# One kernel of four layers: tokens chosen and experts run in one stage, the first layer's products in three float32r passes, the second layer's output products in halves

## The reference, cut to what matters

```
L0:  v = x @ values (16 heads x 64);  cumv = cumsum(v over tokens)
     att = exp((x@aw - max) * temperature);  attn = att * cumv / (att * count + 1e-30)
     op = attn.reshape(S, 1024) @ operator + cond
     res = relu(concat[x, op] @ ff1 + b1) @ ff2 + b2 + x;   x = layernorm(res)
L1:  one-head attention over the normed and FiLM-scaled x, then an MLP of width 1024
L2:  16 heads of 16 features:  out = softmax(q k^T) v, projected, added; then a normed sum
L3:  16 heads of 64 features: attention; then a mixture of 8 experts:
     gate = softmax(tok @ Wgate);  vals, idx = top_k(gate.T, 256)     # each expert picks 256 tokens
     g = layernorm(tok[idx]);  y = gelu(g @ fc1[e] + b1[e]) @ fc2[e] + b2[e]
     tok[idx] += y * vals
```

## Time and profile before

| | us |
|---|---|
| median of 3 runs | 2302.05 (2297.03 to 2305.03) |
| the profiled execution | 2303.45 |
| its span, first to last instruction | 2301.7 |
| mean granted clock of PE over it | 0.897 |
| L0's chunks, about | 36 to 239 |
| L2 heads, about | 698 to 1090 |
| choice, about | 2054 to 2146 |
| experts, about | 2146 to 2302 |

### The profile page before, as it was taken

The page is one execution under the profiler, slowest core; times in us unless marked ns, Lnnn a source line. Parts: engine busy times, 40 slices in busy tenths (PEclk is TensorE's granted clock), DMA queues, the critical chain, the costliest instruction groups (busy, mean ns, idle before and its releaser), DMA issues. The chain is left out here.

```text
span 2301.7 us, 35109 instructions
## 1 busy us (share of the span) xinstructions
PE 1931.4 (84%) x13374; PEld 1181.4 (51%) x13374; DVE 1435.9 (62%) x2490; ACT 1116.1 (48%) x1909; POOL 739.2 (32%) x683
## 2 busy tenths in 40 slices
PE   6998589769747999998389949999999999794776
PEld 3444357658423333332267735555555555483676
DVE  5433453363338989991678857777777777218655
ACT  1111232232211878886167647777777777203242
POOL 2122350074003030000425544444444444103466
PEclk8999799979875999997689979999999999895688
DMA  5000000000133311100238873444444444342153
GB/s 161 0 1 0 16 7 1 22 17 1 37 110 83 89 41 50 47 23 8 80 103 254 261 196 85 111 111 111 111 111 111 111 111 111 97 166 86 36 161 80
DMA packets 196231, 190.99 MB, mean 83 GB/s; under 512 B 64416, under 2 KB 154912, under 8 KB 195808
## 3 DMA queue, kind: packets, MB, share of 16 engines
q1 hardware_dynamic: 192992, 184.56, 30.1%
q0 software_dynamic: 3072, 4.20, 0.9%
HBM read 121.07 MB, written 67.37 MB: 82 GB/s over the span
## 5 line engine op out<-in xcount | busy, mean ns | idle before, releaser
L1302 DVE TENSOR_REDUCE l3h_nmax<-l3h_score 128x1 f32<-128x1024 f32 x256 | 313.5, 1225 | 150.7 <-PE l3h_score L1245 150.6
L1336 POOL TENSOR_SCALAR l3h_prob<-l3h_prob,l3h_inv 128x1024 f32<-128x1024 f32 x256 | 287.0, 1121 | 341.8 <-DVE l3h_inv L1308 341.8
L1528 ACT ACTIVATE l2h_pT<-l2h_score 128x512 f32<-128x512 f32 x512 | 266.1, 603 | 119.2 <-PE l2h_score L1453 117.6
L1495 DVE TENSOR_REDUCE l2h_nm<-l2h_rowb 128x1 f32<-128x1024 f32 x256 | 301.2, 1218 | 35.9 <-PE l2h_rowb L1442 35.9
L1326 ACT ACTIVATE l3h_prob<-l3h_score,l3h_nmax 128x1024 f32<-128x1024 f32 x256 | 285.9, 1117 | 48.7 <-DVE l3h_nmax L1302 13.7
L1268 PE MATMUL l3h_out<-l3h_pT,l3h_vs 128*64 128x512 f32 x1024 | 274.4, 617 | 0.0
L1245 PE MATMUL l3h_score<-l3h_K,l3h_Q 64*128 64x512 f32 x1536 | 249.6, 431 | 23.7 <-DMA l3h_K<-l_k 21.9
L1245 PEld LDWEIGHTS l3h_score<-l3h_K,l3h_Q 64*128 64x128 f32 x1536 | 125.9, 187 | 235.4 <-issue 197.4
L1442 PE MATMUL l2h_rowb<-l2h_K,l2h_Q 48*128 48x512 f32 x512 | 185.9, 477 | 44.2 <-DMA l2h_K<-l_k 29.9
L1453 PE MATMUL l2h_score<-l2h_Q,l2h_K 50*128 50x512 f32 x512 | 204.1, 485 | 4.7 <-ACT l2h_pT L1528 4.7
L1294 ACT ACTIVATE l3h_pT<-l3h_ring 128x512 f32<-128x512 f32 x256 | 152.8, 597 | 101.4 <-PE l3h_ring L1256 100.9
(11 more groups left out here) (377 smaller groups left out, 3583.9 us busy)
## 6 DMA issues: line engine op xcount, KB each, us to landing
l3h_Q<-l_q SPq DMA_DIRECT2D x128, 256.0 KB
l3h_K<-l_k SPq DMA_DIRECT2D x128, 128.0 KB
l_v<-l3qkv_v SPq DMA_DIRECT2D x16, 512.0 KB, 4.3
l_q<-l3qkv_hi SPq DMA_DIRECT2D x16, 512.0 KB, 5.1
l_q<-l3qkv_lo SPq DMA_DIRECT2D x16, 512.0 KB, 4.4
l_k<-l3qkv_hi SPq DMA_DIRECT2D x16, 512.0 KB, 3.5
l_k<-l3qkv_lo SPq DMA_DIRECT2D x16, 512.0 KB, 3.3
l3h_vs<-l_v SPq DMA_DIRECT2D x32, 256.0 KB, 3.2
```

The lines of the kernel that those rows point to most:

```text
L1302: dve.tensor_reduce(self.nmax[:, t % 4:t % 4 + 1], self.score[t % 2][:, :], AX.X, ALU.max, negate=True).then_inc(self.maxes, 1)
L1336: pool.tensor_scalar(self.prob[:, q, :], self.prob[:, q, :], self.inv[:, q:q + 1], self.vscale, ALU.mult, ALU.mult).then_inc(self.scaled, 1)
L1495: dve.tensor_reduce(self.nm[:, mr % 2, at:at + 1], self.rowb[h][:, :], AX.X, ALU.max, negate=True).then_inc(self.maxes, 1)
L1528: act.activation(self.pT[:, g % 4, h, c * C:(c + 1) * C], self.score[v % 3][:, :], ACT.Exp).then_inc(self.exps, 1)
```

## The change

**L0.** `values`, the operator and the half of `ff1` that meets `oT` are split once into high and low parts, `csum` and `oT` once for each chunk, `aT` for each `j` (high part on ACT, low part on POOL); their products run in three passes. PE's order in a chunk is values(j), spread(j), operate(j-2), so the operator product runs in pieces inside the loop over `j`. The small sums for later layers come at j = 3, the second half of the cumulative sums on DVE at n = 5 and 6. `gam` and `bet` are applied chunk by chunk. The loads of the L2 weights move from L0 to `layer1_qkv`. Buffers share storage (`zero`, `sel32`, the raw weights).

**L2 heads.** For tiles 1 to 6, `mix` is done in two halves of 256 columns, one after each phase. Where there are no rows left, PE repeats a row product of the last pair (`again`); nothing reads it.

**Choice and experts** become one stage. One-hots and picks are made for three experts first and the others three experts ahead, inside the loop. Tokens are turned after the second pair of `up`, their high part is written by ACT from PSUM. Weight loads, semaphores and splits are separate for the two matrices, and the splits stand between the gelus. All sixteen biases are loaded once.

```diff
 # layer0, PE
+            for c in range(NC):
+                pe.wait_ge(chi, (c + 1) * KF)
+                pe.wait_ge(clo, (c + 1) * KF)
+                values(c, 0)
+                spread(c, 0)
+                for j in range(1, FT):
+                    values(c, j)
+                    spread(c, j)
+                    if j >= 2:
+                        operate(c, j - 2)
+                    if j == 3:
...
+                for j in range(FT - 2, FT):
+                    operate(c, j)
...
+                for m in range(KF):
+                    for k in range(KF):
+                        pe.matmul(bank[6 + m][:, :], ff1[:, k, m * P:(m + 1) * P], xT[:, k, cc], start=k == 0, stop=False)
+                pe.wait_ge(opc, (c + 1) * 2 * KF)
+                pe.wait_ge(ohi, (c + 1) * KF)
+                for m in range(KF):
+                    for k in range(KF):
+                        for p_, (x, y) in enumerate(PASSES):
+                            mm = pe.matmul(bank[6 + m][:, :], ff1o[x][:, k, m * P:(m + 1) * P], oTp[y][:, k, :],
 # layer0, DVE, in the loop over j
-                    dve.tensor_tensor(aT[:, j, :], bank[2 + n % 2][:, :], rb[:, n % 2, :], ALU.mult).then_inc(ats, 1)
+                    if n >= 2:
+                        dve.wait_ge(alo, n - 1)
+                        dve.wait_ge(ahi, n - 1)
+                    dve.tensor_tensor(aT[:, n % 2, :], bank[2 + n % 2][:, :], rb[:, n % 2, :], ALU.mult).then_inc(ats, 1)
 # NarrowPairs, PE
+            at, w = (part * C // 2, C // 2) if 0 < k < TB - 1 else (0, C)
...
-                    if phase == 0:
-                        mine, kk = (m, k - self.LAG) if k >= self.LAG else (m - 1, k - self.LAG + TB)
-                        if self.there(mine):
-                            mix(mine, kk)
+                    mine, kk = (m, k - self.LAG) if k >= self.LAG else (m - 1, k - self.LAG + TB)
+                    if self.there(mine) and (phase == 0 or 0 < kk < TB - 1):
+                        mix(mine, kk, phase)
 # experts, SP
+            for m in range(2):
+                ew.load(sp, 1, m)
+            for e in range(E):
+                sp.dma_start(b1[:, e, :], columns(w["b1"][e, :]), allow_slow_non_contiguous=True).then_inc(bl, 16)
+            for m in range(2):
+                ew.load(sp, 2, m)
             sp.wait_ge(normed, T)
             sp.dma_start(g["tokn"].rearrange("(t p) d -> p t d", p=P), xn[:, :, :]).then_inc(stored, 16)
             sp.wait_ge(stored, 32)
+            for e in range(E):
+                sp.dma_start(b2[:, e, :], rows(w["b2"][e, :])).then_inc(bl, 16)
+            ew.load(sp, 3, 0)
+            for e in range(3, E):
+                if e + 1 < E:
+                    ew.load(sp, e + 1, 0)
+                ew.load(sp, e, 1)
 # experts, PE
+            tokens(0)
             for e in range(E):
+                up(e)
+                if e >= 1:
+                    down(e - 1)
+                if e + AHEAD < E:
+                    pick(e + AHEAD)
+            down(E - 1)
 # experts, DVE
+                for q in range(PAIRS):
+                    dve.wait_ge(gelus, e * F + 2 * q + 2)
+                    dve.tensor_copy(yp[0][:, e % 2, 2 * q:2 * q + 2, :], y[:, 2 * q:2 * q + 2, :]).then_inc(yhs, 1)
+                    if q == 0 and e >= 1 and e + AHEAD - 1 < E:
+                        indices(e + AHEAD - 1)
+                    if q == 2 and e + 1 < E:
+                        tokens(e + 1)
+                    for i in range(2):
+                        if q < 2 and 2 <= e + 1 < E:
+                            ew.low(dve, e + 1, 0, 2 * q + i)
+                        if q >= 2 and e >= 2:
+                            ew.low(dve, e, 1, 2 * (q - 2) + i)
+                if e + AHEAD < E:
+                    mark(e + AHEAD)
+                if e >= 1:
+                    gated_result(e - 1)
```

More of the change, by code:

```diff
@@ new lines, in spread, with operate @@
+            def spread(c, j):
+                n = c * FT + j
+                if j == 0:
+                    pe.wait_ge(attr, c + 1)
+                    pe.wait_ge(los, c + 1)
+                if n >= 2:
+                    pe.wait_ge(rbc, n - 1)
+                pe.matmul(bank[n % 2][:, :], sel[:, j, :], rhl[:, c % 2, :], start=True, stop=True).then_inc(rbs, 1)
+            def operate(c, j):
+                n = c * FT + j
+                pe.wait_ge(ahi, n + 1)
+                pe.wait_ge(alo, n + 1)
+                if n == 0:
+                    pe.wait_ge(olo, 2)
+                if c >= 1 and j == 0:
+                    pe.wait_ge(f2d, c * TC)
+                for m in range(KF):
+                    for p_, (x, y) in enumerate(PASSES):
+                        mm = pe.matmul(bank[4 + m][:, :], op[x][:, j, m * P:(m + 1) * P], ap[y][:, n % 3, :],
+                                       start=j == 0 and p_ == 0, stop=j == FT - 1 and p_ == 2)
+                mm.then_inc(ops, 1)
@@ L2070, in load @@
+    def load(self, sp, e, m):
         if e >= 2:
[L2071 to L2081 removed]
@@ new lines, in _, with tokens @@
+            for e in range(AHEAD):
+                pick(e)
+            def tokens(e):
+                pe.wait_ge(gl[e % 3], 16 * CT * (e // 3 + 1))
+                if e >= 1:
+                    pe.wait_ge(gts, e * KF)
+                for kf in range(KF):
+                    for h in range(CT):
+                        mm = pe.transpose(tb[:, kf * CAP + h * P:kf * CAP + (h + 1) * P],
+                                          tok[:, e % 3, h, kf * P:(kf + 1) * P], ident[:, :])
+                mm.then_inc(tturned, 1)
@@ new lines, in down @@
+            def down(e):
+                pe.wait_ge(yls, (e + 1) * F)
+                ew.wait_split(pe, e, 1)
+                if e >= 1:
+                    pe.wait_ge(biased, e * CT)
+                for h in range(CT):
+                    for j in range(F):
+                        for p_, (a, b) in enumerate(PASSES):
+                            mm = pe.matmul(db[:, h * D:(h + 1) * D], yp[a][:, e % 2, j, h * P:(h + 1) * P],
+                                           ew.w2T[b][:, e % 2, j * D:(j + 1) * D], start=j == 0 and p_ == 0,
+                                           stop=j == F - 1 and p_ == 2)
+                mm.then_inc(downs, 1)
```

667 lines of the change are left out of this document (342 added, 325 removed).

## The result

The changed kernel takes 2262.8 us (median of 4, 2261.6 to 2264.1) against 2303.3 (median of 4, 2297.0 to 2305.0): ratio 0.983, 95% interval 0.981 to 0.985. 40 us were gained where 86 were forecast, and the time lies outside the range of 2188 to 2250. Its profiled execution took 2263.3 us, with a span of 2261.6.

The account below looks back on a forecast made before the run. It took PE to bound L0, a loop through PE's order the L2 heads, and waits through weight loads the experts. Gains of 28 + 27 + 17.5 + 13.5 = 86 us from 2303.45 gave 2217 us, range 2188 to 2250.

Parts of the forecast that it names:

- L0, 28 forecast: L0: split three-pass products cut PE's work and stalls from 203 to 176 us, plus 1 at the start; bounds 18 and 33.
- Lie beside PE-bound work: Moved L2 loads and chunk-wise gains and shifts: hidden beside PE's work; if uncovered, some 5 us.
- L2 heads, 27 forecast: L2 heads: half mixes gain 18 us while rows run (21.2 to 20.0 a pair) and 9 us behind them.
- the reason given: L2 heads behind the last rows: repeated rows keep PE at work, so the clock stays at 2.4 GHz; 9 us.
- Choice, 17.5 forecast: Choice: one-hots for fewer experts first, so gather at 2126.6 and first up product at 2137, not 2154.34; 17.5 us gained.
- Experts, 13.5 forecast: Experts: the weight load's wait goes; 17.9 us gained on five periods of 18.7, less 4.5; bounds 20 and 0.
- the part on the port: Experts: DVE and POOL hold each other up at the shared port, but already overlap, so waits are counted in busy time.
- period as now: Experts, lower bound of the 13.5 term: periods stay as they are, so 0 us gained.
- the full lock's sum: Experts, rival: port as full exclusive lock, periods 26.4 three times, 22.1 twice, 19 twice; 44 us lost, 2275; chance 0.02.
- The 1.5: Experts: about 1.5 us from the end of DVE's 14.7 us list until the first gelu, making periods of 16.2.
- its sign for L0: What would show the forecast in L0: chunks of 41 us and less on average, with PE busy over 85%.
- its milder form: Experts, rival: the shared port is the bound, periods stay at 18.7; 13.5 us less gained, 2231; chance 0.17.

Follow-up runs that it names:

- e11: Changed kernel with DVE's three splits of operator and feed-forward weights moved into L0's loop, behind its first three products: 2263.5 us, 0.982 of the kernel before.
- e6: Changed kernel with layer 2's four moved loads held back until the first layer 1 stage's own six loads have landed: 2266.7 us, 0.984 of the kernel before.
- e4: Changed kernel without the repeated rows of the last pair in the L2 heads, mixes still in halves: 2269.3 us, 0.983 of the kernel before.
- e18: Kernel before the change, with POOL's 128x2048 subtraction in the L2 heads cut into 16: 2303.2 us, ratio 1.000 to the uncut kernel before.
- e10: Changed kernel with one-hots made one expert earlier and POOL's y_lo subtractions moved to DVE: 2229.7 us, 0.967 of the kernel before.
- e8: Changed kernel with POOL's eight y_lo subtractions an expert made by DVE, two at a time: 2248.3 us, 0.976 of the kernel before.
- e7: Changed kernel with each expert's one-hots made one expert earlier, picks where they were: 2243.1 us, 0.973 of the kernel before.
- e13: Changed kernel with POOL's gathers for expert e+2 issued behind its eight subtractions for e, not ahead: 2261.9 us, 0.980 of the kernel before.
- e15: Changed kernel with POOL's eight 128x256 subtractions an expert made as four of 128x512: 2263.3 us, 0.982 of the kernel before.
- e14: Changed kernel with POOL's 128x2048 subtraction in the L2 heads cut into 16 of 128x128: 2253.9 us, 0.977 of the kernel before.
- e2: Changed kernel with a later expert's 16 one-hots made in four lots, one behind each gelu pair: 2255.1 us, 0.979 of the kernel before.
- e16: Changed kernel with one-hots one expert earlier, y_lo on DVE, POOL's heads subtraction in 16, layer 2's moved loads held back, L0 splits later: 2217.3 us, 0.963.
- e1: Changed kernel with DVE's four casts of y an expert written as two-source max(y, y): 2268.0 us, 0.984 of the kernel before.
- e17: Kernel of e16 with DVE's norm chain of an L0 chunk, and ACT's root, behind the next chunk's first two products: 2212.2 us, 0.959.

## Why the prediction was wrong

**L0, 28 forecast, 19.7 measured.** The mechanism was right; sizes were off. The chunks take 180.3 us against 176: the stalls are smaller than allowed (PE idle 23 us in all, 32 in the sum; 2.8 to 3.1 at a boundary, 4 in the sum), and the work is longer (PE busy 157 us, 144.5 in the sum). The sum priced every product at the full clock; the granted clock was 0.95 on average, and 0.50 to 0.73 in six stretches of 4 us. And the 1 us gained at the start is a loss of 2.8: GpSimd's low rows were costed at their row of before, with nothing of DVE beside them (e11).

**Moved loads, 0 forecast, -2.7.** "Lie beside PE-bound work" is false for their first microseconds: they were moved into a stage whose first products wait for that stage's own loads (e6: 2.0 of the wait are theirs, though the piece as a whole became only 0.7 shorter).

**L2 heads, 27 forecast, 14.6 measured.** The steady part was right: 20.27 us a pair (20.0), and behind the 14th output copy 8.1 gained (9 forecast). The second is luck, not the reason given: e4 keeps the clock without the repeated rows, and in e18 the last pair is 7.4 us shorter with none of the change. It was the profiled execution of before that had lost its clock there. What failed is that the stretch was costed as 14 equal pairs. One stall stands in it, 5.4 us before and 14.1 after (4.9 to 14.1 in other profiles), which no term had: the cast of the row maxima was priced at its few tenths, and it waits for GpSimd's long subtraction. 13 pairs by 0.97 are 12.6, less 8.7 for the stall and 0.2 for one other pair leaves 3.7, and 2.9 were gained at the start.

**Choice, 17.5 forecast and measured.** First gather at 2094.41; first up product 10.8 us behind it (8 to 10 forecast).

**Experts, 13.5 forecast, -9.0 measured, the step that failed most.** From first gelu to first gelu the forecast had 14.5 and 14 us, 16.2 three times and 13.5 twice, 104 in all; measured are 14.2, 18.1, 20.7 three times, 11.8 and 14.1, 120. Behind the last expert's first gelu it took 31.9 us where it took 25.8 before, for which the sum had no term; there stands the pair of splits of 6.56 us, and in e10, with no subtraction on POOL, that end takes 28.0.

The long periods have two causes. Forecast for them were DVE's list of 14.7 and 1.5 until the first gelu; measured are 17.3 and 3.4.

(a) The list. In the part on the port stands "DVE's and POOL's busy time together is 22.1 us an expert now, in a period of 18.7, so they do overlap, and waits are counted in it." They do overlap, but a held instruction counts as busy, so overlap is no evidence against a hold. The 83/8 = 10.4 us an expert had some hold in it already: before, the casts of `y` took 31.9 us in all, against 14.6 in e10 for the same elements in half as many casts. What was put at nothing is what the new order adds. The change put POOL's subtractions between DVE's splits, and the holds of the changed kernel are about 5 us a period (e8, e10). The same work of DVE as before (casts of `y`, splits, sums and gates) takes 97.3 us in place of 81.5. The lower bound of this term, "period as now", was too high, since periods got longer; the full lock's sum, 44 us lost, was too low.

(b) The 1.5. The picks end with the last one-hot, and then 12 passes of the up product run at half the clock (2.77 us), with PE having waited 3.67 us before the picks. e7 takes (b) away, e8 takes (a), and e10 both. Periods of 17.6, 18.4 and 15.3 are what the two parts give.

Two numbers of the prediction do not follow from its own: its lower bounds give 2190 if all four are met, and half of them about 2204; and its sign for L0, chunks of 41 us on average, leaves out the 11 us of sums for later layers (176/4 is 44; measured 45.1). Neither bears on the miss.

The Trainium skill, "SBUF — State Buffer", section Who interferes with whom, says that a DVE instruction in a two-port mode, which a copy or cast can enter, and a GpSimd instruction shut each other out for the whole instruction, and that a DVE instruction with two inputs in SBUF contends with a GpSimd instruction that reads SBUF. I had given this rule, taken in full, a chance of 0.02, and its milder form (periods of 18.7) 0.17; the periods were 20.7. The runs agree with it in the heads (3.61, 1.02 and 0.36 us with the length of POOL's instruction, and 3.58 in the two-source form). What it does not say is the hold over a run of four, six or eight behind a gather or scatter (3.46, 4.83 and 6.56 us; e13, e15), whose cause is not settled: in e14 a run of 16 held the cast for one instruction only, and so did a run of six in e2.

With the five edits of e16 the same change gives 2217.3 us. That this is the time forecast is a coincidence: against before, L0 gives 17.9 us in place of 28, the heads 29.4 in place of 27, and the experts 26.0 in place of 13.5.

## What to carry to other kernels

When work is interleaved, do not price an instruction by a row in which it ran alone: list what GpSimd and VectorE will have side by side, and cut a long GpSimd instruction, or move it, wherever a short one of VectorE feeds PE. That two engines' busy times overlap does not show that neither holds the other. When an engine turns out to be the bound, look for the one wait left in its period and follow it back: here it led round to the engine's own list, and making 16 one-hots one expert earlier (e7) was worth more than any other single edit. A stretch of equal pairs has to be checked for the unequal one.

## What the hardware showed that was not expected

- A short stall can cost four times its length, and the same stall costs different amounts: PE stood still 3.57 us, the granted clock fell to 0.50 and PE, busy 10.00 of 10 us, stayed there some 25 us; 14.1 us in all, and 4.9 in e1, where the clock was back sooner. With whole mixes (21.24 us a pair) it cost 5.4 and 6.4.
- POOL is held by DVE too: low rows 3.82 us in place of 1.25 beside 3 us of DVE's subtractions.
- A small two-source instruction of DVE was held by POOL's arithmetic and not by its indirect transfers alone: index sums took 0.16 us beside scatters and gathers (e7) and 0.4 to 1.3 beside subtractions (e13).
- PE with no gap in its records does not by itself get the higher clock: after the rows-only start of the heads the clock of 0.50 ended some 41 us behind the first row product in the profiles of the changed kernel and of e16, and some 66 and 69 us behind it in those of e17 and e1. In the heads e17 has the code of e16, and e1 that of the changed kernel.
